# Further tile moved in front of expert 7, and each node's lower numbered expert row gathered ahead of the last stores

## The reference, cut to what matters

```python
topk_p, topk_i = jax.lax.top_k(probs, TOP_K)                 # TOP_K = 2, 8 experts
order = jnp.argsort(-score, axis=1)[:, :capacity]            # the 196 best nodes of each expert
dispatch = flat[order]
gate = jax.nn.silu(jnp.einsum('ech,ehi->eci', dispatch, w1))
up = jnp.einsum('ech,ehi->eci', dispatch, w3)
expert_out = jnp.einsum('eci,eih->ech', gate * up, w2) * weight_sel[..., None]
routed = routed.at[order.reshape(-1)].add(expert_out.reshape(-1, h))
out = routed + jax.nn.silu(flat @ s1) * (flat @ s3) @ s2      # then x = x + out
```

## Time and profile before

| what | us |
|---|---|
| median of 3 runs | 1437.44 (1434.43 to 1442.90) |
| the profiled execution, its own time | 1451.11 |
| its span in the profile | 1449.2 |
| busy: PE, DVE, POOL, ACT | 1322.7, 957.3, 649.3, 552.7 |
| mean granted clock of PE | 0.966 |
| PE's share of the chain that ended last | 61% |

### The profile page before, as it was taken

One profiled execution on the slowest core, in us unless ns is written; L12 is line 12 of the kernel. 1 busy time (PEld: TensorE's weight loads), 2 busy tenths in 40 slices (PEclk: granted clock), 3 DMA queues, 4 the chain that ended last, 5 costly groups with the idle time before them and its releaser, 6 DMA issues.

```text
span 1449.2 us, 22946 instructions
## 1 busy us (share of the span) xinstructions
PE 1322.7 (91%) x7588; PEld 1095.9 (76%) x7588; DVE 957.3 (66%) x2154; ACT 552.7 (38%) x650; POOL 649.3 (45%) x569
## 2 busy tenths in 40 slices
PE   7988688999999989999999999999998789989991
PEld 5765588556985569999999999999766569556660
DVE  8967898878687345666665656565267875466663
ACT  0010576232320034545454545454256651223330
POOL 7025777777677553443344324333377830121102
PEclk9999898999999999999999999999999999999995
DMA  7950000020821238777878787878579762347625
GB/s 180 83 127 6 2 2 2 2 66 7 238 65 27 75 134 293 261 275 267 291 254 288 257 285 267 299 254 280 134 264 319 231 185 77 109 133 222 193 96 184
DMA packets 112661, 243.87 MB, mean 168 GB/s; under 512 B 30397, under 2 KB 52090, under 8 KB 112492
## 3 DMA queue, kind: packets, MB, share of 16 engines
q1 hardware_dynamic: 76076, 131.74, 30.5%
q0 software_dynamic: 22432, 72.27, 17.7%
q10 hardware_dynamic: 14080, 38.93, 7.2%
HBM read 202.05 MB, written 45.31 MB: 171 GB/s over the span
## 4 chain that ended last, share of the span: by engine, by line
PE 61%; DVE 19%; DMA 6%; ACT 4%; another core or an unknown queue 4%; issue 3%; POOL 2%; ACTq 1%; DVEq 1%; SPq 0%; POOLq 0%
PE PS L2719 20%; PE PS L2676 6%; PE PS L2926 4%; PE PS L2606 4%; PE PS L2392 3%; PE PS L2937 3%; DMA raw<-in_L_gnn_W_rel 3%; PE PS L2543 3%; DVE wlo L1320 2%; PE PS L2709 2%; DVE e L1320 2%; PE PS L2894 2%; PE PS L2852 2%; DVE e L1599 2%
## 5 line engine op out<-in xcount | busy, mean ns | idle before, releaser
L826 POOL DMA_INDIRECT xg<-xn_dram,xrow x70 | 116.1, 1658 | 287.2 <-DVEq L1529 271.5
L2719 PE MATMUL PS<-whi,xhi 128*128 128x384 f32 x840 | 220.8, 343 | 1.0 <-ACTq L1111 1.0
L2719 PE MATMUL PS<-whi,xlo 128*128 128x384 f32 x840 | 214.4, 336 | 0.0
L2719 PE MATMUL PS<-wlo,xhi 128*128 128x384 f32 x840 | 212.8, 334 | 0.0
L1320 DVE TENSOR_TENSOR wlo<-raw,whi 128x2304 fp32r<-128x2304 f32 x68 | 175.2, 2577 | 39.3 <-ACTq L1094 34.0
L1092 ACT ACTIVATE whi<-raw 128x2304 fp32r<-128x2304 f32 x68 | 145.1, 2134 | 20.1 <-DMA raw<-in_L_gnn_W_rel 11.6
L2719 PEld LDWEIGHTS PS<-wlo,xhi 128*128 128x128 f32 x840 | 151.9, 188 | 0.0
L2719 PEld LDWEIGHTS PS<-whi,xlo 128*128 128x128 f32 x840 | 151.5, 188 | 0.0
L2719 PEld LDWEIGHTS PS<-whi,xhi 128*128 128x128 f32 x840 | 147.9, 188 | 1.3 <-issue 1.3
L1320 DVE TENSOR_TENSOR xlo<-PS,xhi 128x768 fp32r<-128x768 f32 x70 | 67.0, 958 | 121.9 <-ACTq L1103 113.2
L796 POOL DMA_INDIRECT zidxb<-zrow_dram,idxb x80 | 110.7, 1384 | 26.3 <-issue 26.3
(11 more groups left out here) (456 smaller groups left out, 2628.9 us busy)
## 6 DMA issues: line engine op xcount, KB each, us to landing
raw<-in_L_gnn_W_rel SPq DMA_DIRECT2D x68, 1152.0 KB
z_dram<-xn ACTq DMA_DIRECT2D x70, 384.0 KB, 7.4
wroot<-in_L_ffn_w SPq DMA_DIRECT2D x12, 576.0 KB, 7.4
y_dram<-yb ACTq DMA_DIRECT2D x17, 384.0 KB, 3.8
pre<-in_L_ffn_w SPq DMA_DIRECT2D x9, 576.0 KB, 4.7
gw<-in_L_gnn_W SPq DMA_DIRECT2D x2, 2304.0 KB, 27.4
fw<-in_L_ffn_w SPq DMA_DIRECT2D x8, 576.0 KB
fw<-in_L_ffn_w ACTq DMA_DIRECT2D x1, 4608.0 KB, 22.8
```

The lines of the kernel that those rows point to most:

```text
L826: pool.indirect_dma_start(xg[b][j][:, :], None, xn_dram, bass.IndirectOffsetOnAxis(ap=xrow[:, b, j:j + 1], axis=0)).then_inc(x_gathered[b] ...
L2719: mm = pe.matmul(slot(q)[:, s * BANK:s * BANK + HALF], a[:, k, :], wt[:, k, s * HALF:(s + 1) * HALF], start=(k == 0 and part == 0), stop=( ...
```

## The change

- The list runs shared tiles, experts 0 to 6, the further tile, expert 7. So item 14 is now the further tile, and items 15 and 16 are expert 7.
- In `y_dram` the further tiles' rows stand ahead of expert 7's. The part below `LAST2` is thus complete, but for further tiles beyond the first, once item 14 is stored.
- `yrow` and the weights `yw` are no longer ordered by best and second expert but by lower and higher number. The lower of two different numbers is never 7. This costs DVE five small operations more in `row_tables`.
- POOL gathers the five lower rows as soon as items 0 to 14 are stored, and the five higher rows once items 15 and 16 are. It waits for the stores themselves, not for ACT's signal. DVE adds the five lower tiles when all five have landed, then the higher ones as they land (tiles 0 and 1 together).
- SP reads the further tile's expert ahead of its wait.
- PE runs two matmuls whose result nobody reads, between the last `turn_h` and the last outer product.
- Should more further tiles be needed, the lower rows are gathered anew behind them.

```diff
-ITEMS = [(None, t) for t in range(SH)] + [(e, j) for e in range(NE) for j in range(RT)] + [(MORE_OF, 0)]
+ITEMS = ([(None, t) for t in range(SH)] + [(e, j) for e in range(NE - 1) for j in range(RT)] + [(MORE_OF, 0)]
+         + [(NE - 1, j) for j in range(RT)])
-FIRST2 = NE * RT * 128
+FIRST2 = (NE - 1) * RT * 128
 MANY2 = 4 * -(-2 * N * MORE // (4 * ((RT + MORE - 1) * 128 + 1)))
+LAST2 = FIRST2 + MANY2 * 128
...
-            yg = [b[:, :, :].rearrange("p k f -> p (k f)")[:, i * D:(i + 1) * D] for b in w13[1:] for i in range(3)]
-            yg += [b[:, :] for b in fx[1:]] + [sb("yg9", [128, D], f32, g)[:, :]]
+            y_parts = lambda b: [b[:, :, :].rearrange("p k f -> p (k f)")[:, i * D:(i + 1) * D] for i in range(3)]
+            y_lower = y_parts(w13[0]) + [fx[1][:, :], fx[2][:, :]]
+            y_higher = y_parts(w13[1]) + [fx[3][:, :], sb("yg9", [128, D], f32, g)[:, :]]
...
+            sp.wait_ge(f_more_ready, 1)
+            more_of = sp.value_load(f_at[0:1, 0, 0:1], min_val=0, max_val=NE - 1)
             sp.wait_ge(outer_full, SH + RT * (NE - RING + 1))
-            sp.wait_ge(f_more_ready, 1)
-            load_dynamic2(sp.value_load(f_at[0:1, 0, 0:1], min_val=0, max_val=NE - 1), ld_w13[NE % RING], ld_w2e[NE % RING])
+            load_dynamic2(more_of, ld_w13[NE % RING], ld_w2e[NE % RING])
...
+            def gather_lower(t, signal):
+                pool.indirect_dma_start(y_lower[t], None, y_dram[0:LAST2, :],
+                                        bass.IndirectOffsetOnAxis(ap=yrow[:, 0, t:t + 1], axis=0)).then_inc(signal, 16)
+
             pool.wait_ge(f_more_ready, 1)
-            further_tiles(pool, further_gather2, number_of(pool, f_n, MANY2 - 1))
-
+            later = number_of(pool, f_n, MANY2 - 1)
             pool.wait_ge(yrow_ready, 1)
-            pool.wait_ge(y_complete, 1)
-            for n in range(2 * T):
-                pool.indirect_dma_start(yg[n], None, y_dram,
-                                        bass.IndirectOffsetOnAxis(ap=yrow[:, n % 2, n // 2:n // 2 + 1], axis=0)).then_inc(y_gathered[n // 2], 16)
+            pool.wait_ge(y_begun, 16 * (MANY2 // 4))
+            for b in range(2):
+                pool.wait_ge(y_stored[b], 16 * ((NE - 1) * RT // 2 + (b == 0)))
+            for t in range(T):
+                gather_lower(t, y_lower_gathered)
...
+            further_tiles(pool, further_gather2, later, gather_lower_anew)
+
+            for b in range(2):
+                pool.wait_ge(y_stored[b], 16 * (NE * RT // 2 + (b == 0)))
+            for t in range(T):
+                pool.indirect_dma_start(y_higher[t], None, y_dram,
+                                        bass.IndirectOffsetOnAxis(ap=yrow[:, 1, t:t + 1], axis=0)).then_inc(y_gathered[max(t - 1, 0)], 16)
...
-                act.dma_start(y_dram[k * 128:(k + 1) * 128, :], yb[k % 2][:, :]).then_inc(y_stored[k % 2], 16)
+                e, j = ITEMS[n]
+                row = FIRST2 if e == MORE_OF else LAST2 + j * 128 if e == NE - 1 else (e * RT + j) * 128
+                act.dma_start(y_dram[row:row + 128, :], yb[k % 2][:, :]).then_inc(y_stored[k % 2], 16)
...
             def row_tables(a):
+                do(tt(ysel[:, :, :], asg[:, :, :], rev[:, :].unsqueeze(1).broadcast_to([P, T, NE]), ALU.mult))
+                do(dve.tensor_reduce(yw[:, 0, :], ysel[:, :, :], AX.X, ALU.max))
+                do(tt(lower, ysel[:, :, :], yw[:, 0, :].unsqueeze(2).broadcast_to([P, T, NE]), ALU.is_equal))
+                do(tt(higher, asg[:, :, :], lower, ALU.subtract))
...
+                do(dve.memset(frow[:, 0, NE - 1:NE], float(LAST2)))
...
-            further_tiles(dve, further_expert, number_of(dve, f_n, MANY2 - 1))
+            later = number_of(dve, f_n, MANY2 - 1)
+            further_tiles(dve, further_expert, later, lambda: dve.wait_ge(y_lower_gathered, 16 * T + 1))
+            dve.wait_ge(y_lower_gathered, 16 * T)
             for t in range(T):
-                dve.wait_ge(y_gathered[t], 32)
-                for c in range(2):
-                    do(dve.scalar_tensor_tensor(x_res[:, t, :], yg[2 * t + c][0:P, :], yw[:, c, t:t + 1], x_res[:, t, :], ALU.mult, ALU.add))
-                dve.sem_inc(tile_done, 1)
+                step(dve.scalar_tensor_tensor(x_res[:, t, :], y_lower[t][0:P, :], yw[:, 0, t:t + 1], x_res[:, t, :], ALU.mult, ALU.add))
+            step.sync()
+            for t in range(T):
+                dve.wait_ge(y_gathered[max(t - 1, 0)], 32 if t < 2 else 16)
+                dve.scalar_tensor_tensor(x_res[:, t, :], y_higher[t][0:P, :], yw[:, 1, t:t + 1], x_res[:, t, :],
+                                         ALU.mult, ALU.add).then_inc(tile_done, 1)
...
                     last = ITEMS[n - 1][0]
+                    if n == OWN:
+                        for _ in range(2):
+                            pe.matmul(slot(0)[:, 0:HALF], fxT[(n - 1) % 2][:, 0, :], w13[last % RING][:, 0, 0:HALF], start=True, stop=True)
                     pe.wait_ge(hT_ready, n)
```

More of the change, by code:

```diff
@@ L178, in build @@
     xn_dram = nc.dram_tensor("xn_dram", [T * 128, D], f32).ap()
-    y_dram = nc.dram_tensor("y_dram", [FIRST2 + MANY2 * 128, D], f32).ap()
+    y_dram = nc.dram_tensor("y_dram", [LAST2 + RT * 128, D], f32).ap()
     edge_dram = nc.dram_tensor("edge_dram", [T * GE, 4], f32).ap()
@@ L296, in build @@
         y_stored, y_begun, scol_ready, srow_ready, yrow_ready = [sem("y_stored0"), sem("y_stored1")], sem("y_begun"), sem("scol_ready"), sem("srow_ready"), sem("yrow_ready")
-        y_complete, y_gathered, tile_done = sem("y_complete"), [sem(f"y_gathered{t}") for t in range(T)], sem("tile_done")
+        y_complete, tile_done = sem("y_complete"), sem("tile_done")
+        y_lower_gathered, y_gathered = sem("y_lower_gathered"), [sem(f"y_gathered{t}") for t in range(1, T)]
         f_more_ready, f_more_gathered, f_loaded, f_stored, f_freed = sem("f_more_ready"), sem("f_more_gathered"), sem("f_loaded"), sem("f_stored"), sem("f_freed")
@@ L496, in number_of, with further_tiles @@
             return eng.value_load(number[0:1, 0:1], min_val=0, max_val=most)
-        def further_tiles(eng, tile, total):
+        def further_tiles(eng, tile, total, finish=lambda: None):
             with eng.If(total > 0):
@@ L502, in further_tiles @@
                     tile(m)
+                finish()
         def elu_of(t):
@@ L2184, in _ @@
             dve.sem_inc(asg_ready, 1)
-            score = small[:, 7, :, :]
+            score, lower, higher = small[:, 7, :, :], small[:, 4, :, :], small[:, 6, :, :]
             do(dve.scalar_tensor_tensor(score, asg[:, :, :], -1.0, comb1[:, :, :], ALU.add, ALU.add))
@@ L2271, in row_tables @@
                 do(dve.memset(yw_all[:, :, :], 0.0))
-                for c, hot in enumerate((4, 6)):
-                    do(tt(ysel[:, :, :], yrow_f[:, :, :], small[:, hot, :, :], ALU.mult))
+                for c, hot in enumerate((lower, higher)):
+                    do(tt(ysel[:, :, :], yrow_f[:, :, :], hot, ALU.mult))
                     do(dve.tensor_reduce(yw[:, c, :], ysel[:, :, :], AX.X, ALU.add))
@@ L2339, in _ @@
             do(tt(comb1[:, :, :], comb1[:, :, :], small[:, 8, :, :], ALU.mult))
-            for c, hot in enumerate((4, 6)):
-                do(tt(ysel[:, :, :], comb1[:, :, :], small[:, hot, :, :], ALU.mult))
+            for c, hot in enumerate((lower, higher)):
+                do(tt(ysel[:, :, :], comb1[:, :, :], hot, ALU.mult))
                 do(dve.tensor_reduce(yw[:, c, :], ysel[:, :, :], AX.X, ALU.add))
```

7 lines of the change are left out of this document (added).

## The result

The changed kernel takes 1430.86 us, the median of 7 runs (1427.01 to 1433.82), beside 1437.44 of 7 runs of the kernel before (1432.88 to 1442.90). The ratio is 0.9945, with a 95% interval of 0.9922 to 0.9969: 7.9 us less, 4.5 to 11.2 (the two medians themselves are 6.6 apart). The forecast was 11.6 less. The direction is right, the time lies in the range, and the gain is smaller than the sum said.

The account below looks back on a forecast made before the run. PE was taken to bound the kernel until the last outer product, followed by a 30.3 us tail of transfers and additions without PE. The terms summed to -11.6 us from the 1437.44 median, giving 1425.8 us, range 1421 to 1433.

Parts of the forecast that it names:

- row tables: DVE, iteration of item 3: 1.05 us more work, 0.92 of it covered, so +0.15 us on the path.
- weights of the further tile: Before item 14's inner product: their second transfer lands near 1391.35, so PE waits +0.45 us.
- last outer product: PE's final product: two idle-time matmuls shorten the gap to 0.97 us and keep the clock up, -1.97 us.
- last store and hand-over: Between PE's end and POOL's first higher gather: store slowed +0.45 us by lower gathers' end, signal to POOL -0.75 us.
- gathers: POOL's tail: five instead of ten, first start to last landing 9.8 us instead of 19.35, -9.55 us.
- last additions: DVE at the end: one addition, 1.05 us, instead of two, 2.07 us, so -1.0 us.
- output stores: Very end: tiles follow 1.25 us apart, so their stores overlap, +0.6 us (0 to 1.5).
- The rival in which the clock falls all the same: Final PE product: the 0.97 us gap still drops the clock; total -9.6 us, 1427.8 us; chance 0.14.
- the crowding of transfers: Tail: last store 4.9 us, fifth gather's landing 7.6, output stores +1.5; total -6.3, 1431.1 us; chance 0.13.
- The last two: Rivals: lower gathers not early, about -2 us, 1435.4, chance 0.03; further tile's weights late, 1438.8, chance 0.01 (0.02 anything worse).

## Why the prediction was right, and where its size was off

**Right in sign, right in mechanism.** The tail was the place, the lower gathers came early, the clock held, and the loop paid a little. Term by term, forecast and measured, each profile of the changed kernel against the first of the kernel before:

| term | forecast | measured in the first profile | in the second |
|---|---|---|---|
| row tables | +0.15 | +0.44 | +0.45 |
| weights of the further tile | +0.45 | +0.49 (0.25 to 1.09 in nine profiles) | +0.55 |
| last outer product | -1.97 | -1.70 | -1.70 |
| last store and hand-over | -0.30 | +1.22 | +0.55 |
| gathers | -9.55 | -8.48 | -6.07 |
| last additions | -1.0 | -1.05 | -1.05 |
| output stores | +0.6 | +2.44 | +0.25 |
| sum | -11.6 | -6.6 | -7.0 |

The sum is steady between the two profiles, and so is the stretch of the last three terms together (-7.1 and -6.9, where -9.95 was forecast). How it parts into gathers and output stores is not: of these two terms only the sum can be judged.

- **Row tables.** The 1.05 of work on DVE was right: `tail` started 1.04 later against the outer product. The cover was too large by two small readings. In order of time (not in the chain, which I used) PE wanted the product at 1318.30, 0.76 after DVE's end, and 0.12 of that is needed from DVE's end to PE's start. 0.64 of cover leaves 0.40.
- **Weights.** Right, also in how it came about: the second transfer landed 8.8 after its issue, as PE's wait ended.
- **Last outer product.** Right but for 0.27: the 2.58 that I took is the distance to the next product's start, the same product's own row is 2.75, and the last one has nothing behind it that overlaps its end; the 0.1 that is left stays open. And a wrong count on the way: I took two records for the two matmuls where there are four. The gap was 0.30 instead of 0.97, safer than argued. The rival in which the clock falls all the same did not come about in any of eleven profiles.
- **Last store and hand-over.** This is the first term that was off, by 1.5 (0.85 in the second profile). It is two misses that partly cancel: the store took 2.56 more than before, beyond the 2.05 that its bounds allowed, and the hand-over shrank by 1.34, beyond the 0.75 that I took for the most. The store met more than "only the end" of the lower gathers. POOL spends 1.38 to 1.52 on three of the five, because DVE ranks nodes beside them, so that the fifth landed 3.4 after the store's issue, and in these 3.4 the DMA engines were busy 0.84 of the time and moved 280 GB/s. In the kernel with all ten gathers late, with no ranking beside them, the lower ones took 0.95 each. With lower gathers in flight the first higher gather started 4.58 to 6.27 after the store's issue (nine profiles), without them 3.36 and 3.52. The hand-over itself shrank from 1.55 to 0.2. The Trainium skill (DMA: Bandwidth & Descriptors, SWDGE vs HWDGE vs iDMA) says that each engine takes the two kinds of queue by turns; the estimate worked out from it beside the forecast, up to two us more for the store, is near what the nine profiles show (4.3 to 5.4 in place of 2.9 to 3.3), and I should have given it more weight than the quiet end of the earlier trace rows. The turns themselves no profile shows.
- **Gathers.** Off by 1.1 in the first profile, all of it POOL's: two gathers 1.53 and 1.55 beside additions. In the second profile it was 3.5: four gathers of 1.15 to 1.66, 1.4 in all before the fifth, which landed 6.9 after its start where I had 4.8. I had moved the lower additions "under work" and asked only whether DVE was free, not what DVE does to POOL. Five of five kernels whose additions were left out, or taken as rows landed, needed 16.3 to 16.85 from the first higher gather to the end; the changed order with one output queue needed 17.2 to 18.1 in four of five, and 16.4 in one whose store was so late that the additions were nearly over. So of the 17.9 and 18.1 of the changed kernel, where my sum had 15.0, some 1.1 to 1.8 are the additions' doing; the rest is there without them.
- **Output stores.** Off by 1.8 in the first profile and by -0.35 in the second, where the last gather was late instead. I priced each tile's store as before, where SP's ten issues were spread over 14 us. Now ten follow each other within 7, while the last gathers still land. The stretch to 1430.4, at 0.84 busy, suggests that this end is close to full. How much of it is bytes and how much SP's issues, 0.67 each on average, was not settled.

**The rival that came nearest** is the crowding of transfers, 0.13: its sum, -6.3, is nearly the measured -6.6, and both of its outer parts came about, beyond the size it gave (the store 5.4 for 4.9, the output stores +2.44 for +1.5). Its middle part did not in this profile, where the fifth higher gather landed in 4.67, not 7.6; in the second it took 6.9, and there the output stores were quick. I gave it too little, because I priced the crowding by the rows of before, where the gathers are spread out, and took the halved bytes as evidence against it. The bytes behind the last store are halved, but those beside it are new. That the time lay in the range rests on this rival having been taken into it. The last two did not occur: the lower gathers were early in every profile that had them early, and the weights were late by 1.1 at most.

## What to carry to other kernels

When a tail is a chain of transfers, moving half of them under earlier work does not win half of the chain: they collide with the store that everything waits for, and the rest runs into the next limit. Price the moved transfers against what they run beside, and the rest against bytes over the rate seen. Ask of each operation that is moved under cover what it does to its neighbour engine: additions that cost DVE nothing took POOL's gathers from 0.95 to 1.55. And a repair whose stretch gets shorter in a single profile has still to show in the time.

## What the runs showed of the hardware

- A gather that POOL issues while DVE is inside one of its additions, or a ranking operation with two inputs, waits until that operation is over. In the fourteen profiles 52 of the 135 gathers from `y_dram` took 1.03 to 1.72 us. Each had begun 0.12 to 0.81 behind the start of such an operation, and each ended 0.81 to 0.82 behind its end. The other 83 took 0.94 to 0.95, also those during which an addition began, and three that began within 0.07 of an addition's start. With the additions taken out, the higher gathers go back to 0.95. The Trainium skill (SBUF — State Buffer, 🔬 SBUF: two separate sides) says that GpSimd and VectorE share a port pair, and that while VectorE runs an operation with two inputs from SBUF a GpSimd operation that reads SBUF and comes second is kept out until the first is done. These rows agree with that; that the ports are the cause no run here shows.
- The last store, 384 KB, landed in 2.9 to 3.3 in the four profiles with no gather from `y_dram` in flight, and in 4.3 to 5.4 in the nine where five lower ones had gone out just before.
- A single gap of 1.6 in PE's work, behind long full work, was followed by a fall of the granted clock to about 0.5 in three of three profiles, in one of them only half way through the product behind it. Gaps of 0.3 at the same place were not, in eleven of eleven. The length of the gap alone does not decide: elsewhere in these traces a gap of 1.61 (to 335.25 in the changed kernel), one of 1.69 (to 825.50 in the kernel without the idle-time matmuls) and one of 1.55 (to 1274.31 in the kernel with early tables) were followed by a granted clock of 1.00. So the gaps of 1.44 and 1.70 in the earlier trace rows draw no line. That a gap of 0.30 keeps the clock here is shown; the 0.97 of the forecast was never tried.
